# Second cross-attention layer: three of twelve value products as rounded passes, scores three tiles ahead, reciprocals in quarters

## What is computed

```python
q = rmsnorm((h @ Wq).reshape(B, Sq, 16, 128), gq)
k = rmsnorm((ctx @ Wk).reshape(B, 1500, 16, 128), gk)
v = (ctx @ Wv).reshape(B, 1500, 16, 128)
attn = softmax(einsum("bqhd,bkhd->bhqk", q, k) / sqrt(128))
x = x + einsum("bhqk,bkhd->bqhd", attn, v).reshape(B, Sq, 2048) @ Wo
```

## Time and profile before

| what | value |
|---|---|
| median of 3 runs | 2109.33 us (2107.74 to 2110.13) |
| the profiled execution, its own time | 2108.11 us |
| its span, first to last instruction | 2106.3 us |
| granted PE clock, mean | 0.994 |
| PE busy | 2064.8 us (98%) |
| DVE busy | 1575.9 us (75%) |
| ACT busy | 1209.1 us (57%) |
| POOL busy | 1451.7 us (69%) |

### The profile page before, as it was taken

The page is one execution under the profiler, slowest core; times in us unless marked ns, Lnnn a source line. Parts: engine busy times, 40 slices in busy tenths (PEclk is TensorE's granted clock), DMA queues, the critical chain, the costliest instruction groups (busy, mean ns, idle before and its releaser), DMA issues. The chain is left out here.

```text
span 2106.3 us, 28263 instructions
## 1 busy us (share of the span) xinstructions
PE 2064.8 (98%) x8514; PEld 1530.5 (73%) x8514; DVE 1575.9 (75%) x2488; ACT 1209.1 (57%) x4202; POOL 1451.7 (69%) x1094
## 2 busy tenths in 40 slices
PE   7999999999999999999999899999999999999999
PEld 7777777777777777777777467666666666665998
DVE  4689888998889888898886775566666676752577
ACT  3576777677776777677776247444444444432432
POOL 1488888988888888988886155487787878761221
PEclk9999999999999999999999999999999999999999
DMA  3000000000000000000010410111211121101110
GB/s 136 22 24 16 30 30 16 19 26 30 29 17 16 30 30 15 20 26 30 26 41 1 151 41 1 45 57 32 59 30 59 29 59 34 41 0 53 45 48 25
DMA packets 15146, 75.68 MB, mean 36 GB/s; under 512 B 1747, under 2 KB 2115, under 8 KB 13987
## 3 DMA queue, kind: packets, MB, share of 16 engines
q1 hardware_dynamic: 14994, 73.89, 10.8%
HBM read 72.97 MB, written 0.92 MB: 35 GB/s over the span
## 5 line engine op out<-in xcount | busy, mean ns | idle before, releaser
L543 ACT ACTIVATE l_prod_act<-l_prod_act 125x128 f32<-125x128 f32 x1536 | 456.2, 299 | 303.6 <-DVE l_prod_act L729 298.5
L994 POOL TENSOR_TENSOR l_acc<-l_acc,l_probs 125x896 f32<-125x896 f32 x160 | 346.6, 2166 | 68.2 <-ACT l_probs L931 49.8
L639 POOL TENSOR_TENSOR l_prod<-l_prod 125x256 f32<-125x256 f32 x384 | 280.6, 741 | 162.2 <-DVE l_prod L729 161.2
L931 ACT ACTIVATE l_probs<-l_scaled 125x896 f32<-125x896 f32 x192 | 182.8, 952 | 302.3 <-DVE l_scaled L1016 162.5
L1016 DVE TENSOR_TENSOR l_scaled<-l_slots,rk 125x896 f32<-125x896 f32 x192 | 206.9, 1084 | 181.1 <-PE l_slots L1092 181.0
L633 POOL TENSOR_TENSOR l_acc<-l_acc,l_probs 125x896 f32<-125x896 f32 x160 | 340.2, 2126 | 0.0
L543 ACT ACTIVATION_READ_ACCUMULATOR l_prod_act<-l_prod_act 125x1 f32 x1536 | 287.8, 187 | 0.0
L705 DVE SCALAR_TENSOR_TENSOR top<-l_side,mask_bias,top 125x448 f32<-125x448 f32 x330 | 217.3, 658 | 26.7 <-PE l_side L817 18.9
L561 ACT ACTIVATE l_probs<-l_slots,mask_bias 125x448 f32<-125x448 f32 x384 | 219.8, 618 | 1.2
L1090 PE MATMUL l_slots<-l_qhi,l_clo 128*125 128x448 f32 x384 | 203.0, 529 | 0.5
L833 PE MATMUL l_side<-norm_lo,l_chi 128*125 128x512 f32 x384 | 185.1, 482 | 0.1
(11 more groups left out here) (271 smaller groups left out, 4979.9 us busy)
## 6 DMA issues: line engine op xcount, KB each, us to landing
land<-in_ctxT SPq DMA_DIRECT2D x32, 750.0 KB, 4.3
l_nat<-in_ctxN SPq DMA_DIRECT2D x16, 750.0 KB
post_we<-in_experts SPq DMA_DIRECT2D x20, 384.0 KB, 3.0
spare<-in_ctxN SPq DMA_DIRECT2D x8, 750.0 KB
nat<-in_ctxN SPq DMA_DIRECT2D x8, 750.0 KB
spare<-in_wo SPq DMA_DIRECT2D x2, 2048.0 KB, 8.8
spare<-in_wqT SPq DMA_DIRECT2D x4, 512.0 KB, 9.1
mid_fac<-in_factors SPq DMA_DIRECT2D x1, 2048.0 KB, 7.8
```

The lines of the kernel that those rows point to most:

```text
L543: last = act.activation(whole, whole, ACT.Copy, accum_out=msq[:, t, 4 * g + c:4 * g + c + 1])
L639: pool.tensor_tensor(buf[:, :, 0:C // 2], buf[:, :, 0:C // 2], buf[:, :, C // 2:C], ALU.add).then_inc(s.half_sum, 1)
L994: pool.tensor_tensor(acc[:, :], acc[:, :], P[t % NP][:, :], ALU.add).then_inc(s.acc, 1)
```

## The change

In `second_attention`:
- LAG goes from 2 to 3 and NP from 3 to 4.
- The value products of tiles 7, 9 and 11 (counted from 0) are made as three F32R matmuls for each half, from rounded high and low parts of the exponentials and of the context. ACT makes `phi` (`probs_high`) right behind the tile's exp, DVE makes `plo` (`probs_low`) at steps 5, 7 and 9 right behind its scale_scores; ACT's `values_high` and DVE's `values_low` do it once a batch for the three context tiles (384 columns).
- `acc_hi` and `acc_lo` are no buffers of their own any more but `phi[1]` and `plo[1]`.
- `invert` is one reciprocal of 224 columns at each of the steps 1 to 4, and `normalise` one half at step 8 and one at step 10 (both at step 2 before).
- The semaphore increments of y_act and rk_inv, for which nobody waits, are dropped.

```diff
-    LAG, NP = 2, 3
+    LAG, NP = 3, 4
+    SPLIT = [7, 9, 11]
+    tiles_split = slice(7, 12, 2)
...
+        phi = [sb(f"phi{i}", [KT, QW], F32R) for i in range(2)]
+        plo = [sb(f"plo{i}", [KT, QW], F32R) for i in range(2)]
+        acc_hi, acc_lo = phi[1], plo[1]
+        nat_hi = sb("nat_hi", [KT, len(SPLIT), C], F32R)
+        nat_lo = sb("nat_lo", [KT, len(SPLIT), C], F32R)
         acc = sb("acc", [KT, QW], F32)
-        acc_hi, acc_lo = sb("acc_hi", [KT, QW], F32R), sb("acc_lo", [KT, QW], F32R)
...
+            def probs_high(b, t):
+
+                at = SPLIT.index(t)
+                act.wait_ge(s.probs, NT * b + t + 1)
+                if at == 1:
+                    need(act, s.den, b)
+                act.activation(phi[at % 2][:, :], P[t % NP][:, :], ACT.Copy).then_inc(s.p_hi, 1)
+
+            def values_high(b):
+
+                need(act, (s.ld_nat0, s.ld_nat1)[b % 2], 8 * (b + b % 2))
+                need(act, s.pv, NT * b)
+                act.activation(nat_hi[:, :, :], nat[b % 2][:, tiles_split, :], ACT.Copy).then_inc(s.p_hi, 1)
...
+                    if t == 2 and not (isinstance(b, int) and b == 0):
+                        values_high(b)
                     for bt, tt in tile_ahead(LAG, b, t):
                         exp(bt, bt % 2, tt)
+                        if tt in SPLIT:
+                            probs_high(bt, tt)
...
+            values_high(0)
             for i in (0, 2, 4):
                 keep_fold(i)
             exp(0, 0, 0)
             keep_fold(6)
             exp(0, 0, 1)
+            exp(0, 0, 2)
...
+            def probs_low(b, t):
+
+                at = SPLIT.index(t)
+                dve.wait_ge(s.p_hi, (len(SPLIT) + 1) * b + at + 2)
+                dve.tensor_tensor(plo[at % 2][:, :], P[t % NP][:, :], phi[at % 2][:, :].bitcast(F32), ALU.subtract).then_inc(s.p_lo, 1)
+
+            def values_low(b):
+
+                dve.wait_ge(s.p_hi, (len(SPLIT) + 1) * b + 1)
+                dve.tensor_tensor(nat_lo[:, :, :], nat[b % 2][:, tiles_split, :], nat_hi[:, :, :].bitcast(F32),
+                                  ALU.subtract).then_inc(s.p_lo, 1)
+
+            def invert(b, part):
...
-                for half in range(2):
-                    dve.reciprocal(inv[:, half, :], norm_banks[:, half, 0:HALF]).then_inc(s.inv, 1)
+                cols = slice(HALF // 2 * (part % 2), HALF // 2 * (part % 2 + 1))
+                dve.reciprocal(inv[:, part // 2, cols], norm_banks[:, part // 2, cols]).then_inc(s.inv, 1)
...
                     for bt, tt in tile_ahead(LAG, b, t):
                         scale_scores(bt, bt % 2, tt)
+                    if t + 2 in SPLIT:
+                        probs_low(b, t + 2)
                     if t == 0 and not start:
                         sum_low(b - 1)
-                    if t == 1 and not start:
-                        invert(b - 1)
-                    if t == 2 and not start:
-                        normalise(b - 1)
+                    if 1 <= t < 5 and not start:
+                        invert(b - 1, t - 1)
+                    if t == 4 and not start:
+                        values_low(b)
+                    if t in (8, 10) and not start:
+                        normalise(b - 1, t // 10)
...
             query_low(0, 0)
+            values_low(0)
...
-                last = pe.matmul(psO[:, half, 0:HALF], nat[par][:, t, :], P[t % NP][:, cols], start=t == 0, stop=t == NT - 1)
+                if t in SPLIT:
+                    at = SPLIT.index(t)
+                    pe.wait_ge(s.p_lo, (len(SPLIT) + 1) * b + at + 2)
+                    pe.matmul(psO[:, half, 0:HALF], nat_lo[:, at, :], phi[at % 2][:, cols], start=False, stop=False)
+                    pe.matmul(psO[:, half, 0:HALF], nat_hi[:, at, :], plo[at % 2][:, cols], start=False, stop=False)
+                    last = pe.matmul(psO[:, half, 0:HALF], nat_hi[:, at, :], phi[at % 2][:, cols], start=False, stop=t == NT - 1)
+                else:
+                    last = pe.matmul(psO[:, half, 0:HALF], nat[par][:, t, :], P[t % NP][:, cols], start=t == 0, stop=t == NT - 1)
```

More of the change, by code:

```diff
@@ L866, in second_attention @@
     s = semaphores(sem, tag, [
-        "ld_land", "ld_nat0", "ld_nat1", "ctx_hi", "ctx_lo", "q_hi", "q_lo", "scores", "scaled", "probs", "pv", "pv_first", "acc",
-        "acc_hi", "acc_lo", "den", "inv", "o_raw", "o_done", "fold_pe", "fold_act", "fold_dve", "y_pe", "y_act"])
-    LAG, NP = 2, 3
+        "ld_land", "ld_nat0", "ld_nat1", "ctx_hi", "ctx_lo", "q_hi", "q_lo", "scores", "scaled", "probs", "p_hi", "p_lo", "pv", "pv_first", "acc",
+        "acc_hi", "acc_lo", "den", "inv", "o_raw", "o_done", "fold_pe", "fold_act", "fold_dve", "y_pe"])
+    LAG, NP = 3, 4
+    SPLIT = [7, 9, 11]
+    tiles_split = slice(7, 12, 2)
     with ExitStack() as ctx:
@@ L976, in _ @@
                 act.wait_ge(s.y_pe, i + 1)
-                act.activation(land[:, HALF * i:HALF * i + HALF], slots[:, 0, i, 0:HALF], ACT.Copy).then_inc(s.y_act, 1)
+                act.activation(land[:, HALF * i:HALF * i + HALF], slots[:, 0, i, 0:HALF], ACT.Copy)
         @block.gpsimd
@@ L1028, in sum_low, with normalise @@
                 dve.tensor_tensor(acc_lo[:, :], acc[:, :], acc_hi[:, :].bitcast(F32), ALU.subtract).then_inc(s.acc_lo, 1)
-            def invert(b):
+            def probs_low(b, t):
[7 more added lines that the diff above has]
+            def invert(b, part):
                 dve.wait_ge(s.den, b + 1)
                 need(dve, s.o_done, 2 * b)
-                for half in range(2):
-                    dve.reciprocal(inv[:, half, :], norm_banks[:, half, 0:HALF]).then_inc(s.inv, 1)
-            def normalise(b):
+                cols = slice(HALF // 2 * (part % 2), HALF // 2 * (part % 2 + 1))
+                dve.reciprocal(inv[:, part // 2, cols], norm_banks[:, part // 2, cols]).then_inc(s.inv, 1)
+            def normalise(b, half):
                 dve.wait_ge(s.o_raw, 2 * b + 2)
                 o = m.qs[:, bass.ds(b, 1), :, :].rearrange("p o (a h) q -> p (o a) (h q)", a=2)
-                for half in range(2):
-                    dve.wait_ge(s.inv, 2 * b + half + 1)
-                    dve.tensor_tensor(o[:, half, :], inv[:, half, :], o[:, half, :], ALU.mult).then_inc(s.o_done, 1)
+                dve.wait_ge(s.inv, 4 * b + 2 * half + 2)
+                dve.tensor_tensor(o[:, half, :], inv[:, half, :], o[:, half, :], ALU.mult).then_inc(s.o_done, 1)
             def body(b, par, nxt, nxt2):
@@ L1072, in _ @@
             sum_low(B - 1)
-            invert(B - 1)
-            normalise(B - 1)
+            for part in range(4):
+                invert(B - 1, part)
+            for half in range(2):
+                normalise(B - 1, half)
         @block.tensor
@@ L1116, in sums @@
                 pe.wait_ge(s.acc_lo, b + 1)
-                need(pe, s.inv, 2 * b)
+                need(pe, s.inv, 4 * b)
                 if b == 0:
@@ L1237, in between_layers @@
     s = semaphores(sem, tag, ["ld_fac", "ld_bias", "ld_wq", "ld_wk", "ld_g", "ld_next", "ready", "on_act", "on_dve", "fac", "gain",
-                 "zero", "one_r", "bias", "rk_std", "rk_inv", "x_hi", "w_hi", "w_lo", "w_lo1", "sq", "sq_hi", "sq_lo", "ms", "std", "rinv", "r_hi", "r_lo"])
+                 "zero", "one_r", "bias", "rk_std", "x_hi", "w_hi", "w_lo", "w_lo1", "sq", "sq_hi", "sq_lo", "ms", "std", "rinv", "r_hi", "r_lo"])
     with ExitStack() as ctx:
@@ L1406, in _ @@
             for i in range(B):
-                dve.reciprocal(m.rk[:, i, :, :], m.rk[:, i, :, :]).then_inc(s.rk_inv, 1)
+                dve.reciprocal(m.rk[:, i, :, :], m.rk[:, i, :, :])
             for n in range(1, NWQ - 1, 2):
```

## The result

The changed kernel takes 2177.06 us in the median of 4 runs (2173.65 to 2178.47), the kernel before 2109.73 (2107.74 to 2111.02). The ratio is 1.0317, 95% interval 1.0302 to 1.0333: slower by 67 us, or 3.2%. The forecast was slower, 2146 us, with a range of 2112 to 2172. The direction is right; the size is 31 us short and the time lies outside the range.

What follows compares the result with a forecast made beforehand. PE was taken to set the pace, at 34.13 us a batch. Batches 1 to 13 (32.0), batch 14 (0.24), last batch (0.6) and start (3.8) add 36.6 to 2108.11: 2144.7, as a median 2146, range 2112 to 2172.

Steps and rivals of the forecast that it cites:

- The two engines' turns: DVE and POOL instructions on SBUF take turns, each standing for the other's: probs_low about 2.0 us, not 1.09.
- The walk of a batch: One batch followed step by step: normalise's second half stands behind low_parts, PE stands 3.8 us, next values at 36.59.
- V: Time in us, counted from the first values matmul of a batch.
- Start and end: First values at about 1348.3, before 1346.10; batch 0 34.6 us; plus 3.8 in all. Last batch 30.86 us, plus 0.6.
- PE's speed: PE's matmuls counted at full clock, split products at 0.206 us a matmul, also behind the 3.8 us stall.
- The sum: Batches 1 to 13 32.0, batch 14 0.24, last batch 0.6, start 3.8: 36.6 us added to 2108.11.
- PE stays the bound: DVE's new instructions as cheap as sum_low or finding POOL idle, a batch 33.3 us: faster, 2097; chance 0.13.
- One more turn a batch: DVE loses one more turn to POOL each batch, 2.1 us of an add fall on PE: 2175; chance 0.12.
- The second half of normalise slips in before low_parts: At a batch's end that half goes ahead of low_parts, batches 1 to 13 as batch 14: +7.8, 2117; chance 0.12.

Runs made afterwards that it cites:

- Experiment 3: The changed kernel with probs_low, values_low (but for batch 0) and normalise taking their second input from PSUM, numbers wrong: 2096.79 us, 0.9943 of the kernel before.
- experiment 2: The changed kernel with the second half of normalise at step 11, behind the last scale_scores, instead of step 10: 2114.13 us, 1.0023 of the kernel before.
- experiment 5: The changed kernel with low_parts behind POOL's first add of a batch instead of ahead of it, batch 0 as it was: 2117.23 us, 1.0038.
- Experiment 1: The changed kernel with 14 unused F32R matmuls ahead of the first value product of each batch from the second on: 2151.35 us, 1.0201.
- experiment 6: The changed kernel with normalise one batch later at step 0, psO copy and sum_high ahead of the last exp, query_low and values_low moved in batch 0: 2102.44 us.
- experiment 7: The kernel of experiment 6 without the split products: 2101.50 us, 0.9958 of the kernel before.
- experiment 4: The changed kernel without the split products, with its lag, buffers, quarters and normalise places kept: 2113.32 us, 1.0018 of the kernel before.
- experiment 9: The kernel before with only the copy of psO and sum_high ahead of the last exp in ACT's queue: 2103.16 us, 0.9972.

## Why the prediction was right in direction and wrong in size

**The two engines' turns: right.** Experiment 3 shows it without any other change. The mean of probs_low is 84.7 / 48 = 1.76 us where about 2.0 was forecast: POOL often stood for an exp by the time of tile 7, and that probs_low then ran in 1.08. The add behind a probs_low took 2.75 us where 2.9 was forecast (POOL, 1527.13). My sentence that POOL adds without a pause through steps 1 to 10 was too strong. In the batch from 1500.06 values_low took 2.27 us where the walk had 1.6 (14.43 to 16.05) and ended 0.7 late; probs_low of tile 7 took 0.9 less than forecast. That the two misses cancel is luck.

**The walk of a batch: right.** In the batch from 1500.06, step 0 took 6.58 instead of 3.61, 2.97 more. Taking these off, the half of normalise ends at V = 34.01 (33.93 forecast), the last scale_scores starts at 33.94 (33.85), the next values at 36.66 (36.59). I held this point, where low_parts goes ahead of the half, to be the narrowest, with 0.12 for an escape; experiments 2 and 5 show that nearly the whole effect hangs on it.

**Start and end: right.** The first values come at 1350.24, of which 1.95 lie ahead of the second attention (its first instruction on ACT is at 1337.07 instead of 1335.12; in programs with the same code up to there it was anywhere from 1335.0 to 1337.8): 2.19 more, 2.2 forecast. The last batch took 31.06 us to the fold, 30.86 forecast.

**PE's speed: the step that failed.** The sum took each batch's stall of 3.8 us as its own length and every matmul behind it at the full clock: "Batches 1 to 13: 36.59 - 34.13 = 2.46 each, 32.0". Batches 1 to 14 took 537.72 us (1386.69 to 1924.41) instead of 477.78, 59.9 more and not the sum's 32.2. Step 0 of batches 2 to 14, 13 times, takes 26.4 us more in all than 3.61 each. So 26.4 of the missing 27.7 are the clock's, and 1.3 are the walk's own, 0.1 a batch. Experiment 1, with the clock held, agrees: its 14 batches take 513.48, 24.2 less, although its batch 14 is 35.81 us, some 1.4 over the changed kernel's 36.11 less the 1.7 of the slow step 0: PE idles only 1.33 us there, less than the added matmuls take. The forecast had the stall and its length; it put the price of the slow matmuls behind it at nothing, without a reason. Batch 0 is the same at small: 36.45 us, 34.6 forecast, with matmuls at 0.37 us behind the stall of 2.2 us for query_low that the forecast had placed:

```profile
1376.63 0.57 PE L1135 MATMUL l_slots<-l_qlo,l_chi 128*125 128x448 f32 x1
1377.00 0.57 PE L1136 MATMUL l_slots<-l_qhi,l_chi 128*125 128x448 f32 x1
```

With both added, 36.6 + 27.7 + 1.9 = 66.2, plus the 1.95 ahead of the block, 68.2 of the 69.9 us between the profiled executions. Of the rest, 1.7 us, 0.2 lies in the last batch and 1.4 behind the fold (220.6 us against 219.2), where the stretch at the lower clock is twice as long; the windows, first of the kernel before, then of the changed one:

```profile
1961.00:1965.00 4.00, 4.00 (x14) 3.59 (x13) 0.59 (x3) 2.14 (x3) 0.00 (x0) 0.57 0.00 0
```

```profile
2028.00:2036.00 8.00, 8.00 (x32) 7.31 (x32) 1.46 (x4) 3.00 (x5) 0.00 (x0) 0.57 0.00 0
```

**The rivals.** "PE stays the bound" gave 2097 for DVE instructions that do not wait; experiment 3, in which probs_low, values_low and normalise do not wait, took 2096.8. "One more turn a batch" gave 2175, near the measured time, and would have been right by accident: PE waited for low parts only twice, 2.8 us in all. "The second half of normalise slips in before low_parts" did not happen, but its 2117 is close to what experiments 2 and 5 measured without that meeting (2114.1 and 2117.2).

## What to carry to other kernels

Give an idle stretch of PE, new in each round of a loop, a second price for the slow matmuls behind it: here 3.6 us of idle time cost 1.6 to 3.0 us more each time. Ahead of moving a DVE instruction with two SBUF inputs, look which POOL instruction reads SBUF at the new place and how long it is; behind it in DVE's queue there should be nothing that PE needs. And try the order of queues before the arithmetic: the copy of psO and sum_high moved one place up in ACT's queue won 6 us on the kernel before, 4.2 of them in this block, and the three split tiles beside it won nothing (experiments 6 and 7) until the last batch was left plain (2095.8 against 2101.5; 4.4 of these 5.7 us lie between the first value product and the fold, the others outside this block).

## What the runs showed of the hardware that was not expected

PE's clock fell to half behind a single idle stretch of 3.6 us, in batches in which PE was otherwise busy nearly without a pause, and also behind one of 2.2 us in batch 0 and of 2.2 us in the last batch of experiment 6; behind the 0.8 us of experiments 1 and 2 and the 1.3 us of experiment 5, once a batch, and one of 1.5 us in experiment 4, it did not. With 14 matmuls a batch whose results nobody reads, the same program was 26 us faster.

In the last block it fell in some executions and not in others of the same code (experiment 9).

A POOL instruction that has been issued and stands for DVE is listed with its waiting time: low_parts 4.19 us behind probs_low, 3.39 alone. Two SBUF inputs made the difference between 1.08 us and up to 2.45 us for one and the same subtraction; with the second input in PSUM it was 1.07 to 1.09 at any time.
